# Rows of seven tiles turned and added by DMAs instead of TensorE and VectorE

## The chip, the cores and the metric

One Trainium2 chip, one of its cores. The metric is the device time of one execution of the whole program in microseconds, as the median of several runs.

## What is computed

The input `x` is 128 by 128 by 128 (batch, node, feature). Two residual blocks follow one another, each `layernorm(x + f(x))` over the last axis, with no gain or shift. The first `f` is a two-layer graph network with batch norms. The second `f` mixes the nodes twice with `adj`, and then runs LSTMs over windows of the node axis:

```python
for p in range(1, MAX_SKIP + 1):          # p = 1, 2, 3, 4
    nw = Tv // p
    wins = h[:, :nw * p, :].reshape(Bv * nw, p, Hd)
    last = _lstm_last(Wih[p - 1], Whh[p - 1], bih[p - 1], bhh[p - 1], wins)
    idx = jnp.arange(nw) * p + (p - 1)
    h = h.at[:, idx, :].set(last.reshape(Bv, nw, Hd))
return h
```

So each period p overwrites every p-th row of `h`, and what period 4 leaves is added to the residual, normalized over the 128 features and written.

## The kernel before, in words

The first 400 us compute the first block and the two graph layers of the second. This case is about what follows. The LSTM is cut into 129 units, each one step `s` of a tile of four windows of a period `p` (`Unit(p, tile, s)`). A unit has 512 columns (a few have 256), three gates if it is the first step, else four. The order of the units is a list written out by hand (`LATE`, L84), and every engine walks the same list by slot number `n`:

- **TensorE** (L851 to L854): per gate three matmuls of 512 columns for the input and three more for the state (weights and values are split into a high and a low half in half precision), L678 to L692, into a ring of six banks. Behind unit `n` come the turns that the table `TURNS` gives for slot `n`.
- **ScalarE** (L986 to L988): the gates of unit `n` (L919), then the tanh of its cell (L926).
- **VectorE** (L1296 to L1323): the low half of unit n-1 (L1164), the cell of unit `n` (L1140 for a first step, else L1143, L1145, L1147), the end work that `ADDS` and `MOMENTS` give for slot `n`, then the hidden state (L1154) and its high half (L1159). Each instruction waits in this order.

The values of the last period end up in `hist`: features on the partitions, and for each of 128 times and 128 batch entries a high and a low half in half precision. The output wants the batch on the partitions, so the rows have to be turned. The end is done in 8 tiles of 16 times. Of every four times in a tile, three (`r` = 0, 1, 2) are not rewritten by period 4, so they can be taken as soon as periods 2 and 3 have written them; the fourth (`r` = 3) is the result of the tile's last unit `4.tile.3`. Per tile and `r`, four times are handled at once:

```python
nc.tensor.matmul(acc, hist[:, 0, t, :], ident16[:], start=True, stop=False)
done = nc.tensor.matmul(acc, hist[:, 1, t, :], ident16[:], start=False, stop=True)
```

These are L820 and L821, four times each, into bank 6 or 7 (for `r` = 3 four transposes at L818). VectorE then adds the bank to the residual rows in the tile's buffer (`end_add`, L1227), takes statistics of each row (`end_row_stats`, L1234) and, when the three first rows or the fourth are complete, turns them into mean and variance (`end_moments`, L1177 to L1184). GpSimd follows in the order of `MOMENT_ORDER`: a power for the reciprocal deviation (L545), then a subtract and multiply per row of 128 (L555), 12 rows for the piece `(tile, 0)` and 4 for `(tile, 3)`. The two last pieces, of tiles 6 and 7, are scaled by VectorE (L1253). SyncE writes each piece when it is scaled (L487) and, as there are six tile buffers for eight tiles, loads tiles 6 and 7 when tiles 0 and 1 are written (L472).

`ln_slots` (L159) lays this out. In slots, the end work of before stands at:

```
turns (0,0..2) 61-63   (2,0..2) 76-78    (1,0..2) 80-82    (3,0..2) 89-91
      (4,0..2) 97-99   (5,0..2) 110-112  (6,0..2) 116-118  (7,0..2) 120,121,123
      (0,3) 96  (1,3) 108  (3,3) 114  (2,3) 115  (4,3) 122  (5,3) 126  (6,3) (7,3) 128
add, statistics: one slot behind the turn
```

## Time and profile before

| | |
|---|---|
| median of 3 runs | 754.97 us (754.64 to 755.01) |
| the profiled execution's own time | 754.89 us |
| its span, first to last instruction | 753.1 us |
| TensorE busy | 736.5 us (98%) |
| VectorE busy | 658.2 us (87%) |
| ScalarE busy | 537.7 us (71%) |
| GpSimd busy | 316.5 us (42%) |

The profiled execution's time is 1.8 us more than its span, for what lies around the first and last instruction. The page counts a matmul as busy until its modelled end, and matmuls are pipelined, so a busy share of TensorE doesn't tell by itself whether it waits; its timeline and the list of waits do.

### The profile page before, as it was taken

What the parts mean: (1) busy time and instruction counts of PE and PEld (TensorE: products, weight loads), DVE (VectorE), ACT (ScalarE), POOL (GpSimd) and SP (SyncE); (2) the same over time, 40 slices, a digit from 0 to 9 for tenths busy, and PEclk for the clock granted to TensorE, in tenths of its full rate; (3) what the DMA queues carried; (4) which work ended last, traced back from release to release, by engine and by line L of the source; (5) the groups of instructions that cost most, each with busy time, mean ns of one, the idle gap of its engine ahead of it and who ended that gap; (6) DMA issues with size and microseconds to landing.
All of it is one profiled execution on the core that took longest, in us unless ns stands there. A gap on an engine that the chain in (4) does not pass through costs nothing.

```text
span 753.1 us, 11475 instructions
## 1 busy us (share of the span) xinstructions
PE 736.5 (98%) x3996; PEld 425.2 (56%) x3996; DVE 658.2 (87%) x1400; ACT 537.7 (71%) x870; POOL 316.5 (42%) x286
## 2 busy tenths in 40 slices
PE   8999999999999999998999999999999999999994
PEld 7777544777777677673444444444444444554542
DVE  6888787899898999758998799889999898899987
ACT  4877998567778677659888686786676767666652
POOL 1000000168788787800000002600981946239986
PEclk9999999999999999999999999999999999999997
DMA  5642400033423324105200000100100121021012
GB/s 160 189 140 86 112 2 0 1 83 86 113 77 93 105 65 112 31 28 221 114 1 2 0 1 1 43 0 1 39 34 14 43 70 43 1 70 57 14 57 84
DMA packets 64605, 45.06 MB, mean 60 GB/s; under 512 B 1658, under 2 KB 63524, under 8 KB 63524
## 3 DMA queue, kind: packets, MB, share of 16 engines
q1 hardware_dynamic: 64548, 44.33, 19.2%
q8 instruction: 32, 0.52, 0.3%
q14 instruction: 25, 0.20, 0.1%
HBM read 27.55 MB, written 16.78 MB: 59 GB/s over the span
## 4 chain that ended last, share of the span: by engine, by line
PE 71%; DVE 18%; ACT 7%; issue 2%; SPq 1%; DMA 0%; POOL 0%; POOLq 0%; DVEq 0%
PE ps L678 10%; PE ps L687 10%; PE ps L679 10%; PE ps L646 7%; PE ps L683 7%; PE ps L692 7%; PE ps L684 7%; ACT work L919 4%; PE ps L585 4%; DVE ln_stats L1190 3%; DVE ring L1171 2%; DVE store L1218 2%; DVE ring L1207 2%; PE ps L602 2%; PE ps L601 2%
## 5 line engine op out<-in xcount | busy, mean ns | idle before, releaser
L919 ACT ACTIVATE work<-ps,gate_bias 128x512 f32<-128x512 f32 x449 | 282.6, 680 | 91.4 <-PE ps L692 57.6
L678 PE MATMUL ps<-store,wih 128*128 128x512 f16 (+1 forms) x443 | 166.7, 376 | 2.3 <-ACT work L919 2.3
L679 PE MATMUL ps<-store,wih 128*128 128x512 f16 (+1 forms) x443 | 166.7, 376 | 0.0
L687 PE MATMUL ps<-store,wih 128*128 128x512 f16 (+1 forms) x443 | 156.0, 376 | 0.0
L545 POOL TENSOR_TENSOR end_mv<-end_mv,minus_half 128x12 f32<-128x12 f32 (+1 forms) x16 | 31.0, 1940 | 256.0 <-DVE end_mv L1184 256.0
L536 POOL TENSOR_SCALAR ring<-ring,ln_mv 128x128 f32<-128x128 f32 x112 | 113.0, 1021 | 2.8 <-POOL ln_mv L524 2.7
L1154 DVE TENSOR_TENSOR work<-work 128x512 f32<-128x512 f32 (+1 forms) x129 | 88.2, 684 | 22.4 <-ACT work L926 22.4
L926 ACT ACTIVATE work<-store 128x512 f32<-128x512 f32 x97 | 60.5, 623 | 53.0 <-DVE store L1147 36.4
L683 PE MATMUL ps<-store,whh 128*128 128x512 f16 (+1 forms) x248 | 93.2, 376 | 0.0
L684 PE MATMUL ps<-store,whh 128*128 128x512 f16 (+1 forms) x248 | 93.1, 376 | 0.0
L692 PE MATMUL ps<-store,whh 128*128 128x512 f16 (+1 forms) x248 | 93.0, 376 | 0.0
L555 POOL TENSOR_SCALAR ring<-ring,end_mv 128x128 f32<-128x128 f32 x72 | 85.7, 1202 | 1.4 <-POOL end_mv L545 1.4
L1164 DVE TENSOR_TENSOR store<-work,store 128x512 f16<-128x512 f32 (+1 forms) x121 | 81.9, 677 | 1.4 <-ACT store L952 1.4
L678 PEld LDWEIGHTS ps<-store,wih 128*128 128x128 f16 x443 | 43.3, 98 | 53.1 <-issue 8.2
L687 PEld LDWEIGHTS ps<-store,wih 128*128 128x128 f16 x443 | 43.3, 98 | 50.9 <-DVE store L1164 0.3
L679 PEld LDWEIGHTS ps<-store,wih 128*128 128x128 f16 x443 | 43.3, 98 | 48.3 <-issue 5.0
L519 POOL TENSOR_TENSOR bn_rstd<-mean_var,minus_half 128x1 f32<-128x1 f32 x3 | 1.7, 555 | 133.6 <-DVE mean_var L1098 77.2
L555 POOL TENSOR_SCALAR store<-store,end_mv 128x128 f32<-128x128 f32 x48 | 55.0, 1157 | 1.1 <-POOL end_mv L545 1.1
L870 ACT ACTIVATE store<-ps,vec 128x512 f32<-128x512 f32 x64 | 40.4, 684 | 13.4 <-PE ps L591 13.4
L1143 DVE TENSOR_TENSOR work<-work 128x512 f32<-128x512 f32 (+1 forms) x62 | 42.3, 683 | 8.5 <-ACT work L919 7.5
L1145 DVE TENSOR_TENSOR store<-work,store 128x512 f32<-128x512 f32 (+1 forms) x62 | 42.2, 680 | 7.4 <-ACT work L919 7.2
L1057 DVE BATCH_NORM_STATS2 st<-store 128x6 f32<-128x512 f32 x64 | 41.1, 684 | 8.5 <-ACT store L870 8.3
(136 smaller groups left out, 1284.4 us busy)
## 6 DMA issues: line engine op xcount, KB each, us to landing
ring<-in_x_dram SPq DMA_DIRECT2D x32, 256.0 KB, 3.0
ring<-in_x_dram SPq DMA_DIRECT2D x16, 512.0 KB, 5.3
x_scratch<-ring SPq DMA_DIRECT2D x16, 512.0 KB, 3.5
ring<-x_scratch SPq DMA_DIRECT2D x5, 1024.0 KB, 4.8
out_dram<-ring SPq DMA_DIRECT2D x5, 768.0 KB, 3.5
store<-x_scratch SPq DMA_DIRECT2D x3, 1024.0 KB, 14.1
out_dram<-store SPq DMA_DIRECT2D x3, 768.0 KB, 3.5
out_dram<-ring SPq DMA_DIRECT2D x5, 256.0 KB, 2.3
```

The source lines that it names most:

```text
L536: last = nc.gpsimd.tensor_scalar(row, row, mv[:, 1, b:b + 1], mv[:, 4, b:b + 1], ALU.subtract, ALU.mult)
L555: last = nc.gpsimd.tensor_scalar(row, row, mv[:, 1, k:k + 1], mv[:, 4, k:k + 1], ALU.subtract, ALU.mult)
L678: nc.tensor.matmul(acc(j), w_hi, x_hi, start=True, stop=False)
L679: nc.tensor.matmul(acc(j), w_lo, x_hi, start=False, stop=False)
L683: nc.tensor.matmul(acc(j), w_hi, h_hi, start=False, stop=False)
L684: nc.tensor.matmul(acc(j), w_lo, h_hi, start=False, stop=False)
L687: last = nc.tensor.matmul(acc(j), weights(wih, j)[0], x_lo, start=False, stop=u.first)
L692: nc.tensor.matmul(acc(j), weights(whh, j, 1)[0], h_lo, start=False, stop=True)\
L919: nc.scalar.activation(acts[:, n % 2, gate, 0:u.cols], ps[:, gate_bank(q), 0:u.cols], ACT.Tanh if gate == G else ACT.Sigmoid, bias=gate_bi ...
L926: nc.scalar.activation(tanh_c[:, n % 2, 0:UNITS[n].cols], unit_cell(n), ACT.Tanh)\
L1154: nc.vector.tensor_tensor(hid, hid, tanh_c[:, n % 2, 0:u.cols], ALU.mult).then_inc(hid_done, 1)
L1164: nc.vector.tensor_tensor(unit_output(u, 1), columns(acts[:, n % 2, O, :], u), unit_output(u, 0), ALU.subtract).then_inc(lo_done, 1)
```

## The change

The rows 0 to 2 of tiles 0 to 6 (`MOVED`) no longer go over TensorE and VectorE. For each such tile SyncE issues eight DMAs with a transpose, two halves times four groups of three times, each of 128 by 384 numbers in half precision, into a buffer `h_rows`. It waits for the units that write the rows and for both adds of the tile moved before. GpSimd waits for the four DMAs of the high half and issues a DMA that adds them to the tile's rows, waits for the four of the low half and for its first adding DMA, and issues a second one. VectorE's statistics wait for both.

`h_rows` lies over `minus_c` and `u1_bias`, which only the graph layers use; the buffer for the three is one bank larger. The slots of after:

```
move 0..6 at 59, 69, 76, 83, 92, 99, 113     add (GpSimd) one slot later
statistics (0,0..2) 68-70    (1,0..2) 78-80    (2,0..2) 85-87    (3,0..2) 92-94
           (4,0..2) 101-103  (5,0..2) 108,110,111   (6,0..2) 119-121
turns      (7,0..2) 120,121,123, and the fourth rows where they were
```

GpSimd and SyncE now walk the slots too. In a slot GpSimd first issues the adds and then does the powers and scalings, so the adds of tile 1 stand ahead of the scaling of tile 0 (both slot 70), those of tile 2 (77) ahead of tile 1's (80), those of tile 3 (84) ahead of tile 2's (87), those of tile 4 (93) ahead of tile 3's (94). SyncE issues the writes of a piece four slots behind its statistics (`OUT_DELAY`), behind that slot's moves. The 12 rows of the piece `(6, 0)` are scaled by ScalarE, four each behind the tanh of slots 123, 124 and 125; GpSimd only computes their power and the product of mean and reciprocal deviation, with the mean's sign turned.

```diff
+MOVED = range(P // T_TILE - 1)
+ROWS_ADDED, STATS_DELAY = 6, 9
...
+        start = max(written + 1, start + ROWS_ADDED + 1)
+        put(moves, start, tile)
+        put(lands, start + 1, tile)
+        wanted.append((start + (STATS_DELAY if tile < MOVED[-1] else ROWS_ADDED) - 1, tile))
...
+OUT_DELAY = 4
+BY_SCALARE, BY_VECTOR = [(6, 0)], MOMENTS[len(UNITS) - 1]
+POOLED = [piece for piece in MOMENT_ORDER if piece not in BY_SCALARE and piece not in BY_VECTOR]
+SCALES = {max(n for n in STATS if (6, 2) in STATS[n]) + 2 + r: (6, r) for r in range(3)}
...
-        minus_c = sb("minus_c", [P, CB, P])
-        u1_bias = sb("u1_bias", [P, CB, P])
+        turned = sb("turned", [P, 3 * BANK])
+        minus_c, u1_bias = (turned[:, k * BANK:(k + 1) * BANK].rearrange("p (b n) -> p b n", b=CB) for k in range(2))
+        h_rows = turned[:].bitcast(F16).rearrange("p (s k d) -> p s k d", s=2, d=P)
...
+            def move_rows(tile):
+                n = MOVE_ORDER.index(tile)
+                sp.wait_ge(lo_done, halves_through(max(NUMBER[v] for v in sources(Unit(4, tile, 0)))))
+                wait(sp, h_added, 32 * n)
+                for s in range(2):
+                    for m in range(CB):
+                        t = tile * T_TILE + 4 * m
+                        sp.dma_start(h_rows[:, s, 3 * m:3 * m + 3, :],
+                                     hist[:, s, t:t + 3, :].rearrange("p t b -> p (t b)"),
+                                     transpose=True).then_inc(h_moved[s], 16)
...
+            for n in range(N_EARLY, len(UNITS) + OUT_DELAY):
+                for tile in MOVES.get(n, ()):
+                    move_rows(tile)
+                for piece in MOMENTS.get(n - OUT_DELAY, ()):
+                    write_rows(piece)
...
+            def add_rows(tile):
+                n = MOVE_ORDER.index(tile)
+                rows = first_rows(x1_tile[tile % X1_RING])
+                pool.wait_ge(x1_loaded[tile % X1_RING], 16 * (tile // X1_RING + 1))
+                for s in range(2):
+                    pool.wait_ge(h_moved[s], 16 * CB * (n + 1))
+                    wait(pool, h_added, 16 * (2 * n + s))
+                    nc.gpsimd.dma_start(rows, h_rows[:, s, :, :].rearrange("p (m r) d -> p m (r d)", r=3), accum_op=ALU.add).then_inc(h_added, 16)
...
+                if piece in BY_SCALARE:
+                    nc.gpsimd.tensor_tensor(mv[:, 2, cols], mv[:, 1, cols], mv[:, 4, cols], ALU.mult)\
+                        .then_inc(end_offset, 1)
+                    return
...
+            for n in range(N_EARLY, len(UNITS)):
+                for tile in LANDS.get(n, ()):
+                    add_rows(tile)
+                for piece in MOMENTS.get(n, ()):
+                    scale_rows(piece)
...
+            def end_scale(tile, r):
+                piece = (tile, 3 if r == 3 else 0)
+                act.wait_ge(end_offset, BY_SCALARE.index(piece) + 1)
+                for m in range(CB):
+                    row = x1_tile[tile % X1_RING][:, 4 * m + r, :]
+                    k = r * CB + m
+                    last = nc.scalar.activation(row, row, ACT.Identity, bias=end_mv[:, tile, 2, k:k + 1],
+                                                scale=end_mv[:, tile, 4, k:k + 1])
+                if r == moment_rows(piece).stop - 1:
+                    last.then_inc(end_scaled_act, 1)
...
             for n in range(N_GROUPED, len(UNITS)):
                 gates(n)
                 tanh_cell(n)
+                if n in SCALES:
+                    end_scale(*SCALES[n])
...
-                dve.wait_ge(end_added, ADD_ORDER.index((tile, r)) + 1)
+                if (tile, r) in TURN_ORDER:
+                    dve.wait_ge(end_added, TURN_ORDER.index((tile, r)) + 1)
+                else:
+                    dve.wait_ge(h_added, 32 * (MOVE_ORDER.index(tile) + 1))
...
-                    for tile, r in ADDS.get(n, ()):
-                        end_add(tile, r)
+                    for tile, r in STATS.get(n, ()):
+                        if (tile, r) in TURN_ORDER:
+                            end_add(tile, r)
                         end_row_stats(tile, r)
```

## Rows read from the trace of the kernel before

**Rows 1.** The page, part 1: busy us (share of the span) and instructions of each engine.
```profile
PE 736.5 (98%) x3996; PEld 425.2 (56%) x3996; DVE 658.2 (87%) x1400; ACT 537.7 (71%) x870; POOL 316.5 (42%) x286
```

**Rows 2.** Stages: us, busy (count) of PE PEld DVE ACT POOL, PEclk, DMA, GB/s.
```profile
448.00:550.00 102.00, 102.00 (x522) 48.20 (x520) 94.20 (x190) 72.21 (x115) 40.37 (x30) 1.00 0.05 16
550.00:650.00 100.00, 100.00 (x521) 48.90 (x519) 88.72 (x176) 69.62 (x113) 53.18 (x41) 1.00 0.11 38
650.00:741.00 91.00, 91.00 (x497) 45.68 (x495) 84.12 (x208) 57.12 (x92) 71.55 (x60) 1.00 0.13 41
sum 293.00, PE 293.00 PEld 142.78 DVE 267.03 ACT 198.96 POOL 165.11; mean PE 97.67 PEld 47.59 DVE 89.01 ACT 66.32 POOL 55.04
```

**Rows 3.** Timeline of TensorE: start us, duration us, line, operation, count.
```profile
450.70 0.38 PE L692 MATMUL ps<-store,whh 128*128 128x512 f16 x1
450.91 0.22 PE L820 MATMUL ps<-ident,store 128*128 128x128 f16 x1
...
451.36 0.38 PE L678 MATMUL ps<-store,wih 128*128 128x512 f16 x1
...
741.33 0.60 PE L818 MATMUL ps<-ident,work 128*128 128x128 f32 x4
```

**Rows 4.** List of waits from 440 us: who waited for whom, us, times, longest.
```profile
PE ps L818 <- DVE work L1154: 2.5, 1, 2.5
...
PEld ps L692 <- DVE store L1164: 0.4, 2, 0.2
```

**Rows 5.** Groups by line from 440 us: count | busy us, mean ns | idle before.
```profile
L555 POOL TENSOR_SCALAR ring<-ring,end_mv 128x128 f32<-128x128 f32 x72 | 85.7, 1202 | 1.4 <-POOL end_mv L545 1.4
...
L1227 DVE TENSOR_TENSOR ring<-ps,ring 128x512 f32<-128x512 f32 x20 | 13.6, 681 | 0.0
L820 PE MATMUL ps<-ident,store 128*128 128x128 f16 x96 | 13.3, 219 | 0.0
L821 PE MATMUL ps<-ident,store 128*128 128x128 f16 x96 | 13.3, 219 | 0.0
```

**Rows 6.** Timeline of GpSimd and of SyncE's queue.
```profile
466.12 2.66 POOL L545 TENSOR_TENSOR end_mv<-end_mv,minus_half 128x12 f32<-128x12 f32 x1 [147.07 <-DVE end_mv L1184]
468.96 14.06 POOL L555 TENSOR_SCALAR ring<-ring,end_mv 128x128 f32<-128x128 f32 x12 [0.18 <-POOL end_mv L545]
...
483.05 0.39 SPq L487 DMA_DIRECT2D out_dram<-ring  x1
...
662.05 0.34 SPq L472 DMA_DIRECT2D ring<-x_scratch  x1
```

**Rows 7.** DMA issues: count, KB each, median us from issue to landing.
```profile
store<-x_scratch SPq DMA_DIRECT2D x3, 1024.0 KB, 14.1
out_dram<-store SPq DMA_DIRECT2D x3, 768.0 KB, 3.5
...
work<-in_L_gnn_bg_dram SPq DMA_DIRECT2D x1, 64.0 KB, 3.0
```

**Rows 8.** Timeline of VectorE: starts of the cells of units 69, 85, 92, 108, 121.
```profile
483.31 0.69 DVE L1143 TENSOR_TENSOR work<-work 128x512 f32<-128x512 f32 x1 [0.43 <-ACT work L919]
...
546.97 0.69 DVE L1143 TENSOR_TENSOR work<-work 128x512 f32<-128x512 f32 x1
...
577.35 0.69 DVE L1140 TENSOR_TENSOR store<-work 128x512 f32<-128x512 f32 x1
...
644.84 0.69 DVE L1143 TENSOR_TENSOR work<-work 128x512 f32<-128x512 f32 x1 [1.15 <-ACT work L919]
...
703.80 0.69 DVE L1143 TENSOR_TENSOR work<-work 128x512 f32<-128x512 f32 x1
```

**Rows 9.** ScalarE's L941, from 147 us: ns min/median/max.
```profile
L941 ACT ACTIVATE ring<-ring,ln_mv x14: 477/479/494, 147.0 to 155.1; 128x128 f32<-128x128 f32 x14
```

**Rows 10.** Timeline of ScalarE and VectorE, units 126 to 128.
```profile
728.27 1.85 ACT L919 ACTIVATE work<-ps,gate_bias 128x512 f32<-128x512 f32 x3
...
735.06 0.69 ACT L919 ACTIVATE work<-ps,gate_bias 128x512 f32<-128x512 f32 x1 [0.46 <-PE ps L692]
...
737.25 0.68 DVE L1164 TENSOR_TENSOR store<-work,store 128x512 f16<-128x512 f32 x1
```

More of the change, by code:

```diff
@@ L156, in scaled_through @@
     return scaled_rows(min(g, 1), 7) + max(g - 1, 0)
+MOVED = range(P // T_TILE - 1)
+ROWS_ADDED, STATS_DELAY = 6, 9
 def ln_slots():
-    turns, adds, moments = {}, {}, {}
+    moves, lands, turns, stats, moments = {}, {}, {}, {}, {}
     end = len(UNITS) - 1
@@ L170, in ln_slots @@
         fixed[NUMBER[Unit(4, tile, 3)] + 1] = tile
-    wanted = []
+    wanted, start = [], 0
     for tile in range(P // T_TILE):
-        ready = max(NUMBER[v] for v in sources(Unit(4, tile, 0))) + 2
-        wanted.append((max(ready, NUMBER[Unit(4, tile, 0)]), tile))
-    places, free = [(at, (tile, 3)) for at, tile in fixed.items()], 0
+        written = max(NUMBER[v] for v in sources(Unit(4, tile, 0)))
+        if tile not in MOVED:
+            wanted.append((max(written + 2, NUMBER[Unit(4, tile, 0)]), tile))
+            continue
+        start = max(written + 1, start + ROWS_ADDED + 1)
+        put(moves, start, tile)
+        put(lands, start + 1, tile)
+        wanted.append((start + (STATS_DELAY if tile < MOVED[-1] else ROWS_ADDED) - 1, tile))
+    places, free = [(at, (tile, 3)) for at, tile in fixed.items()], {}
     for at, tile in sorted(wanted):
         for r in range(3):
-            at = max(at, free)
+            at = max(at, free.get(tile in MOVED, 0))
             while at in fixed:
@@ L357, in resnorm_gnn_kernel @@
         x1_loaded = [sem(f"x1_loaded{k}") for k in range(X1_RING)]
+        h_moved = [sem(f"h_moved{s}") for s in range(2)]
+        h_added = sem("h_added")
+        end_offset, end_scaled_act = sem("end_offset"), sem("end_scaled_act")
         h_turned, end_added, end_stats_done, end_step, end_var, end_rstd, end_scaled, tail_scaled = (
@@ L1212, in bias_u1 @@
                 nc.vector.tensor_tensor(u1[:, h * CB:(h + 1) * CB, :].rearrange("p b n -> p (b n)"), ps[:, U1[h], :],
[L1213 removed]
+                                        turned[:, BANK:2 * BANK], ALU.add).then_inc(u1_copied, 1)
             def gnn_lo(g):
@@ L1238, in end_moments, with end_scale @@
                 tile, rows = piece[0], moment_rows(piece)
[L1239 removed]
+                dve.wait_ge(end_stats_done, CB * (STAT_ORDER.index((tile, rows.stop - 1)) + 1))
                 cols = slice(rows.start * CB, rows.stop * CB)
                 moments(end_stats[:, tile % 2, :, :, :].rearrange("p r m s -> p (r m) s")[:, cols, :],
[L1242 to L1244 removed]
+                        end_mv[:, tile, :, cols], end_step, 4 * n, end_var,
+                        sign=-1.0 if piece in BY_SCALARE else 1.0)
+            def end_scale(tile, r):
+                piece = (tile, 3 if r == 3 else 0)
                 n = MOMENT_ORDER.index(piece)
[L1246 removed]
                 dve.wait_ge(end_step, 4 * (n + 1))
                 dve.wait_ge(end_rstd, n + 1)
[L1249 to L1255 removed]
+                for m in range(CB):
+                    row = x1_tile[tile % X1_RING][:, 4 * m + r, :]
+                    k = r * CB + m
+                    last = nc.vector.tensor_scalar(row, row, end_mv[:, tile, 1, k:k + 1],
+                                                   end_mv[:, tile, 4, k:k + 1], ALU.subtract, ALU.mult)
+                if r == moment_rows(piece).stop - 1:
+                    last.then_inc(tail_scaled, 1)
             residual(0, 0)
@@ L1309, in _ @@
                 else:
-                    for tile, r in ADDS[end][:-1]:
+                    for tile, r in STATS[end][:-1]:
                         end_add(tile, r)
@@ L1314, in _ @@
                     hidden_hi(n)
-            for tile, r in ADDS[end]:
-                if (tile, r) == ADDS[end][-1]:
+            for tile, r in STATS[end]:
+                if (tile, r) == STATS[end][-1]:
                     end_add(tile, r)
@@ L1321, in _ @@
                         end_moments(piece)
-            for piece in TAIL:
-                end_scale(piece)
+            for tile, r in TAIL:
+                end_scale(tile, r)
 DEG_STEP = 9
```

52 lines of the change are left out of this document (22 added, 30 removed).

## The prediction

> **What bounds the kernel now.** I read the page first, for shares: TensorE is busy for 98% of the span, VectorE for 87% [rows 1]. A share is an average, so the next view is the table by stage over 448 to 741 us, the only stretch that the change touches: TensorE is busy without a break in every stage, at a granted clock of 1.00, which is the 2.4 GHz level, while VectorE stands at 89 to 92% and ScalarE at 63 to 71% [rows 2]. A busy TensorE may still hide waits, so I then read its own timeline: matmuls of 512 columns start every 0.215 us, and next to them a turned row takes its place in the same row of starts, from 450.91 us to the next gate matmul at 451.36 us [rows 3]. The list of waits confirms it: from 440 us on TensorE's matmuls waited once, for 2.5 us, and that is the last turn of all, behind the final unit; its weight loads waited for tenths [rows 4]. So in this stretch the end moves by what leaves TensorE's stream, one for one, as long as the other engines still deliver on time. Behind 741.33 us stand the tail of turn, add, statistics, power, scaling and write, 11.8 us, which the change leaves as it is.
>
> **What is removed.** Seven tiles times three rows are 21 turns, each of eight matmuls of 128 columns. L820, one of their two lines, counts 96 for eight tiles (L821 the same), so 84 of each go [rows 5]. One turn costs 451.36 - 450.91 = 0.45 us, and 21 of them 9.4 us. (Not eight times the mean of the group, 219 ns: that holds the pipeline's latency, the distance of starts is the price.) On VectorE the 21 adds from PSUM go, of 0.68 us each: 14.3 us [rows 5]. That shortens no sum by itself, since VectorE isn't the bound, but it loses more than TensorE does, so it stays ahead. Tile 7, the fourth rows of all tiles and all statistics stay.
>
> **What is added on SyncE.** Per tile eight transposing DMAs of 96 KB. No transposing DMA stands in the trace, so I bound one: from below by the issue of a plain one, 0.39 us; from above by a whole landing of a 64 KB transfer, 3.0 us, as if each waited for the last [rows 6, 7]. I take i = 1.5 us, between the two, as a descriptor stream that turns data should cost more than an issue and a queue should hide part of the landing: 12 us a tile. What else SyncE does is now threaded between them: each tile's write comes at the earliest four slots behind its statistics, and tile 6's eight transposes (12 us) stand ahead of a write and of tile 7's load, which was issued at 662.05 us for a use behind 703.80 us [rows 6, 8]. Even 12 us later and landing in 14.1 us it is 15 us early. So this queue has a price only if turned rows land late.
>
> **What is added on GpSimd.** Per tile two adding DMAs from half to single precision into the tile. Each moves 768 KB of destination in and out. The nearest row is the 768 KB write, landed after 3.5 us; the farthest the 1,024 KB load that queued behind others, 14.1 us [rows 7]. I take 5 us, and 1 us of GpSimd for each issue (bounds: the 0.39 us issue and the 2.66 us of its power instruction [rows 6]). GpSimd waits in place, first for the turned rows, then for the first add; behind it stand the power and scaling of the tile before, 2.66 + 0.18 + 14.06 = 16.9 us [rows 6], and behind that on SyncE the write of that tile and the next tile's move. This is the one loop that can become late, and its tightest case is tile 2. Tile 1's move starts when unit 68 is written, inside slot 69: its cell starts at 483.31 us [rows 8], less three removed turns (1.3), plus 2.5 us of that slot's VectorE work, 484.5 us. Then eight transposes (8i), landing (2), the second issue (1), scaling of tile 0 (16.9), its write's issue (0.4), eight transposes (8i), landing (2), the second add (5): tile 2 is complete at 511.8 + 16i. VectorE wants it in slot 85: 546.97 us [rows 8], less nine turns (4.0), plus 2.1 us of cell work, 545 us. So it is in time while i is below (545 - 511.8) / 16 = 2.1 us; at i = 1.5 it is 9 us early. Tile 5 repeats the pattern from 577.35 us to 644.84 us [rows 8]: 577.35 - 5.4 + 2.5 + 27.3 + 16i against 644.84 - 6.7 + 2.1, so i up to 2.4 us. Tiles 0, 1, 3 and 4 don't wait for a scaling ahead of their move, or do so with more room. So at i = 1.5 the cost is nothing, and the cover is these 9 us.
>
> How the Trainium skill prices it stands by itself. "VectorE: DVE Perf Modes", The three transpose paths, gives a 128 by 128 block of two-byte numbers 390 ns on TensorE and 1,309 ns through the DMA crossbar, which speaks against this change: three such blocks one after another would be 3.9 us a DMA, far above 2.1. "DMA: Bandwidth & Descriptors", Latency and other measured facts, gives 261 GB/s for transposing DMAs, by which 96 KB would be 0.4 us, far below. No row here decides between them.
>
> **What is added on ScalarE.** Tile 6's 12 rows, four behind the tanh of each of slots 123 to 125. The same instruction at L941 took 0.479 us [rows 9], so 1.9 us a slot, 5.7 us in all. In the last of them ScalarE would end at 730.2 us instead of 728.3; the three gates that took it 1.85 us from 728.27 us [rows 10] and the fourth then run back to back to 732.8. By the gate at 735.06 us it is still some 0.6 us late. That gate leads to the cell of unit 127 and, behind it, to the low halves at 737.25 us [rows 10], for which the weight load of TensorE's last unit waits already, 0.2 us of the 0.4 that L692 waits for L1164 [rows 4]: 0.6 us comes back onto the path. TensorE's six banks hide the rest. GpSimd loses those 12 rows (14.4 us at 1.20 us each [rows 5]), which pays for part of its new waits.
>
> **The sum.** -9.4 + 0.6 = -8.8 us against the profiled execution, 754.89 us with a span of 753.1 us: 746.1 us. The median shown is 754.97 us, 0.08 above it, so the forecast is 746.2 us. 0.2% (1.5 us) is about what a measurement of this kernel can tell from no change.
>
> **Rivals.**
> 1. *The turned rows come late.* It decides from i = 2.1 us on. Each further 0.1 us holds tile 2 by 1.6 us, as VectorE waits in its own order and TensorE runs dry after its six banks. At the upper bound i = 3.0 tile 2 is late by 511.8 + 48 - 545 = 15 us, tile 5 by 10 to 16, tiles 4 and 6 by a few: some 38 us against 9.4 gained, so about 783 us. For it: two queues take turns in one loop, and GpSimd, busy for 165 of 293 us already, is held for most of the rest. Against it: bigger plain transfers are issued in 0.39 us [rows 6], and the DMA engines are busy for 5 to 13% [rows 2]. Chance 0.15. (The skill's 1,309 ns a block, from "VectorE: DVE Perf Modes", would be this rival at i = 3.9: tile 2 alone 29 us late, the time above 800 us, as an estimate. It is part of the 0.15.)
> 2. *Part of the gain is given back.* The chain gate, cell, tanh, hidden, halves becomes the bound here and there once TensorE's stream is denser: VectorE's 92% of 448 to 550 us leaves 7.8 us of 102 [rows 2]; or i is 2.1 to 2.4 and tile 2 or 5 holds VectorE for 1 to 5 us. 748 to 752 us. For it: the low halves of unit 126 already come a little late [rows 4, 10]. Against: VectorE loses 14.3 us, TensorE 9.4. Chance 0.15.
> 3. *Nothing comes of it.* The end is held by something that the turns only filled. Against it stands a TensorE without a gap from 448 to 741 us [rows 2, 4]. About 755 us, chance 0.04.
>
> The forecast has 0.66, from 745.3 (no ScalarE price) to 747.5 us.
>
> **How the numbers follow.** Faster by over 0.2%: the forecast and the second rival, 0.81. Within: 0.04. Slower: 0.15. The range goes from 744.6 us, a turn's price with the rounding of its starts (0.45 against 0.43 to 0.48), to 752 us, the far end of the second rival; the slow rival and the empty one, 2 in 10, are left out.
>
> **What the profile after should show.** L820 and L821 x12 each; L1227 x11; TensorE's stretch without a gap, ending at about 732.5 us instead of 741.33; 56 transposing DMAs issued by SyncE at under 2.1 us each; no wait of VectorE's statistics (L1234) for a DMA; ScalarE's 12 new instructions at 0.48 us; the tail again 11.8 us. Wrong would be: statistics that wait for GpSimd's DMA in slots 85 or 108, TensorE idle behind it, or a granted clock below 1.00 in a stage.

## The result, and the profile after

| | before | after |
|---|---|---|
| median (range, runs), us | 754.76 (754.64 to 755.3, 7) | 751.98 (748.01 to 752.72, 7) |
| the profiled execution's own time | 754.89 us | 748.24 us |
| its span | 753.1 us | 746.4 us |

The ratio of the means is 0.9946, with a 95% interval of 0.9935 to 0.9956: 4.1 us faster (2.8 us by the medians), where 8.6 us were forecast. And there is no single time after: executions lie anywhere from 748.0 to 752.7 us, while those of before agree within 0.7 us. The profile of after comes from one of the fastest, so it shows only part of the loss; profiles of the slower ones were taken later.

The page of after, part 1, answers [rows 1], and the stages answer [rows 2] (columns as there).

```profile
PE 726.6 (97%) x3828; PEld 414.8 (56%) x3828; DVE 644.1 (86%) x1379; ACT 540.2 (72%) x882; POOL 315.2 (42%) x289
```
```profile
448.00:550.00 102.00, 101.94 (x473) 45.95 (x472) 91.83 (x180) 76.22 (x121) 37.84 (x28) 1.00 0.41 81
550.00:650.00 100.00, 100.00 (x486) 47.40 (x484) 87.16 (x192) 68.51 (x111) 67.69 (x57) 1.00 0.47 106
650.00:741.00 91.00, 83.75 (x428) 40.93 (x426) 80.41 (x205) 58.37 (x101) 64.01 (x55) 0.99 0.32 84
```

168 matmuls and 21 VectorE instructions went, so the change does what it says. The DMA engines, busy for 5 to 13% before, stand at 32 to 47%. TensorE's last unit is done earlier by 741.33 - 734.64 = 6.7 us [rows 3], which is the whole gain of the span, and the tail behind it is 11.8 us as before:

The timeline of TensorE of after (columns as in [rows 3]).

```profile
702.18 0.66 PE L878 MATMUL ps<-ident,work 128*128 128x128 f32 x4 [2.14 <-DVE work L1227]
...
734.64 0.60 PE L878 MATMUL ps<-ident,work 128*128 128x128 f32 x4
```

21 turns at 0.45 us would be 9.4 us. Adding up the gaps between starts of TensorE's rows from 448 to 734 us gives 2.6 us (0.23 near 504 us, 2.30 at 702.18 us, 0.06 elsewhere), and 9.4 - 2.6 = 6.8. So everything that was removed came, and in this execution one gap took most of the loss. The waits of after from 440 us answer [rows 4].

```profile
PE ps L878 <- DVE work L1227: 4.6, 2, 2.4
...
DVE end_stats L1310 <- DMA ring<-turned: 3.1, 2, 2.9
...
DVE end_stats L1310 <- DMA store<-turned: 1.1, 1, 1.1
```

The first line holds the old wait of the last turn (2.45 us) and the new one of 2.14 us. The others are what the prediction called the sign of an error: statistics that wait for GpSimd's adding DMA (the profile names the tile's buffer now ring, now store). Its place is in the timeline of VectorE of after, the first statistics of tiles 2 (slot 85) and 6 (slot 119), and the hidden state behind them.

```profile
543.18 0.87 DVE L1310 BATCH_NORM_STATS2 end_stats<-ring 128x6 f32<-128x128 f32 x4 [0.28 <-DMA ring<-turned]
...
691.18 0.87 DVE L1310 BATCH_NORM_STATS2 end_stats<-ring 128x6 f32<-128x128 f32 x4 [2.86 <-DMA ring<-turned]
...
701.44 0.68 DVE L1227 TENSOR_TENSOR work<-work 128x512 f32<-128x512 f32 x1
```

Follow the 2.86 us back. The timelines of SyncE's queue and of GpSimd and, in the last line, the chain of waits of after:

```profile
663.67 11.73 SPq L510 DMA_TRANSPOSE turned<-store  x8
...
675.45 1.35 SPq L522 DMA_DIRECT2D out_dram<-ring  x1
...
679.70 0.34 SPq L493 DMA_DIRECT2D ring<-x_scratch  x1
```
```profile
672.27 1.26 POOL L588 DMA_DIRECT2D ring<-turned  x1
...
679.36 1.28 POOL L588 DMA_DIRECT2D ring<-turned  x1 [5.82 <-DMA turned<-store]
```
```profile
679.36 11.80 DMA ring<-turned
```

Tile 6's second add is issued at 679.36 us, tile 7's load of 1 MB at 679.70 us. A write of 768 KB is issued right behind, at 680.09 us. The add lands after 11.8 us. The stage says how full the 16 DMA engines are (0.91, at 240 GB/s):

```profile
680.00:692.00 12.00, 12.00 (x63) 5.72 (x62) 8.45 (x17) 8.16 (x13) 10.96 (x11) 1.00 0.91 240
```

VectorE is 2.86 us late in slot 119 and has two more statistics to do in slots 120 and 121, so the hidden state of unit 121, which tile 4's last turn reads, comes late, and TensorE waits for it.

### The profile page after: what moved, and what is told of

Same layout as the page of the kernel before. It is cut to its first block, busy times and chain, and to the rows that moved or that the text cites. A ratio compares the mean times of both kernels' runs of the same rounds, so it can differ in the third digit from the quotient of the medians.

```text
span 746.4 us, 11167 instructions
## 1 busy us (share of the span) xinstructions
PE 726.6 (97%) x3828; PEld 414.8 (56%) x3828; DVE 644.1 (86%) x1379; ACT 540.2 (72%) x882; POOL 315.2 (42%) x289
## 4 chain that ended last, share of the span: by engine, by line
PE 60%; DVE 21%; ACT 7%; DMA 4%; SPq 3%; issue 3%; POOL 0%; POOLq 0%; DVEq 0%
PE ps L739 8%; PE ps L740 8%; PE ps L748 8%; PE ps L707 7%; PE ps L744 5%; PE ps L753 5%; PE ps L745 5%; ACT work L979 4%; PE ps L646 4%; DVE ln_stats L1263 3%; SPq L510 3%; DVE work L1227 2%; DVE store L1291 2%; DVE ring L1244 2%; DVE ring L1280 2%
## 5 line engine op out<-in xcount | busy, mean ns | idle before, releaser
L588 POOL DMA_DIRECT2D ring<-turned x8 | 10.6, 1319 | 198.5 <-DMA turned<-store 190.5
L610 POOL TENSOR_SCALAR ring<-ring,end_mv 128x128 f32<-128x128 f32 x60 | 71.3, 1200 | 1.3 <-POOL end_mv L596 1.3
L610 POOL TENSOR_SCALAR store<-store,end_mv 128x128 f32<-128x128 f32 x48 | 50.6, 1066 | 1.1 <-POOL end_mv L596 1.1
```

Of the source, the lines that this page charges most:

```text
L610: last = nc.gpsimd.tensor_scalar(row, row, mv[:, 1, k:k + 1], mv[:, 4, k:k + 1], ALU.subtract, ALU.mult)
```

## The experiments

Differences of one microsecond matter here, so each kernel has 4 to 6 runs beside those of the kernel before, except where fewer are named. All medians are in us.

### The changed kernel again, and the DMAs alone taken out

r1_again and r2_again are the changed kernel as it is.

> The changed kernel once more, unedited. Its seven times lie in two heaps, 748.0 to 749.5 us and 752.0 to 752.7 us, and only one of the first heap has a trace. Theory A (late rows: the statistics of tiles 2, 5 and 6 wait for the adding DMAs, whose landing varies): where the time is near 752 us the profile shows VectorE's statistics waiting some 4 us longer in total than the 4.2 us seen, and a longer hole in TensorE. Theory B (ScalarE's twelve scalings hold the last gates): the time near 752 us shows the same waits for DMAs and more idle TensorE in slots 124 to 128. Theory C (the chain gate, cell, hidden state is too slow for the denser stream): small gaps all over. Median between 748 and 752.7 us by all three.

Measured: 750.92 (750.25 to 752.54, 5), ratio 0.9945 (0.9933 to 0.9958), span 749.3. Its profile shows more of what that of after shows: the statistics of tile 5 in slot 108 wait 4.1 us and not 1.1. Slots 124 to 128 have no gap, and small gaps all over aren't there either, so theories B and C have nothing for them. One part of theory A is wrong: the landing doesn't vary. Tile 5's second add takes 9.3 us in after and 9.6 in r1_again; what differs is when it is issued. r2_again ran later:

> The changed kernel, unedited, beside the mended ones on one chip: 748 to 752.7 us, 2.5 to 6 us above loads apart in every run.

Measured: 749.19 (748.05 to 753.64, 6), ratio 0.9931 (0.9912 to 0.995). One run lies above the range and no run between 750.03 and 753.64 us.

e1_no_moves takes out both kinds of DMA and the waits for them:

```diff
-                wait(sp, h_added, 32 * n)
...
-                        sp.dma_start(h_rows[...], hist[...], transpose=True).then_inc(h_moved[s], 16)
...
-                for s in range(2):
-                    pool.wait_ge(h_moved[s], 16 * CB * (n + 1))
-                    wait(pool, h_added, 16 * (2 * n + s))
-                    nc.gpsimd.dma_start(rows, h_rows[...], accum_op=ALU.add).then_inc(h_added, 16)
...
-                    dve.wait_ge(h_added, 32 * (MOVE_ORDER.index(tile) + 1))
+                        dve.wait_ge(x1_loaded[tile % X1_RING], 16 * (tile // X1_RING + 1))
```

> The 56 transposing and 14 adding DMAs are left out, with the waits for them, so seven tiles' first three rows miss their LSTM part; everything else stands as in the changed kernel. This is the ceiling of the change. Theory A: TensorE has no hole from 448 us to its last unit, VectorE's statistics wait for nothing, the whole 9.4 us come, less at most 0.6 for ScalarE: 745.3 to 746.1 us, and the times lie in one heap within 0.5 us. Theory B: 748 us or more, with the loss in slots 124 to 128. Theory C: 748 us or more, with gaps all over.

Measured: 746.26 (746.18 to 746.85, 4), ratio 0.9884 (0.9869 to 0.9899), span 744.1. From 440 us on TensorE's matmuls wait once, for the last turn (waits of e1_no_moves), and the last stage is full again at a DMA share of 0.14:

```profile
PE ps L867 <- DVE work L1216: 2.5, 1, 2.5
```
```profile
650.00:732.00 82.00, 82.00 (x419) 40.10 (x418) 72.93 (x178) 56.80 (x97) 55.93 (x47) 1.00 0.14 46
```

The whole loss lies in the DMAs or in what waits for them, and the spread over several us is gone with them. That 746.26 us meets the forecast of 746.2 us to the tenth is partly luck: the forecast holds 0.6 us for ScalarE that no gap shows, and 0.4 us of this time lies outside the span (746.28 - 744.1 = 2.2 us in its profile, where before has 1.8).

### Which DMA, and beside what

e4_small_loads leaves the moves and the adds and shrinks the loads of tiles 6 and 7:

```diff
-                    load_x1(tile + X1_RING)
+                    late = tile + X1_RING
+                    sp.dma_start(x1_tile[late % X1_RING][:, 0:1, :], x1_dram[:, late * T_TILE:late * T_TILE + 1, :])\
+                        .then_inc(x1_loaded[late % X1_RING], 16)
```

> Tiles 6 and 7 load one of their sixteen rows (64 KB instead of 1,024 KB), so the rest of their residual is missing; nothing else is changed. Theory A1 (the second adding DMA of tiles 5 and 6 is slow because it shares the DMA engines with these two loads, issued 1.2 us and 0.3 us beside it): the second adds of tiles 5 and 6 land in 6 to 7 us instead of 9.3 and 11.8, the waits of slots 108 and 119 shrink from 1 to 4 and 2.9 us to under 1 us each, the hole of 2.3 us goes: 746.5 us, within 0.5 of the kernel without moves (746.26). Rival A2 (the adds are slow because GpSimd issues them late, behind its scalings, and transposes and writes load the engines): both waits stay over 1 us, time over 748 us.

Measured: 745.67 (745.6 to 745.78, 4), ratio 0.9875 (0.9859 to 0.9892). Tile 6's second add alone, from issue to landing (view by source line), and the load beside it (DMA issues from 660 to 700 us, columns as in [rows 7]), after and then e4_small_loads:

```profile
DMA to landing us min/median/max: 11.8/11.8/11.8
...
ring<-x_scratch SPq DMA_DIRECT2D x1, 1024.0 KB, 6.1
```
```profile
DMA to landing us min/median/max: 7.6/7.6/7.6
...
ring<-x_scratch SPq DMA_DIRECT2D x1, 64.0 KB, 1.9
```

Tile 6's second add takes 7.6 us and not 11.8, tile 5's 5.7 and not 9.3, and of the statistics' waits one of 0.3 us is left. Nothing but the two loads was made smaller, and all adds, moves and writes stayed.

e5_loads_apart does it with the whole computation: each late load goes where no add is under way. For that the writes come one slot earlier too (`OUT_DELAY`), so this run by itself doesn't tell the loads from the writes; e4_small_loads, which leaves the writes in their slots, does.

```diff
-OUT_DELAY = 4
+OUT_DELAY = 3
...
-                if piece[1] == 3 and tile + X1_RING < TILES:
+                if piece[1] == 3 and 0 < tile < TILES - X1_RING:
...
+                if n == 109:
+                    sp.wait_ge(h_added, 32 * 6)
+                    sp.wait_ge(out_written[0], 32)
+                    load_x1(X1_RING)
```

> The two loads are moved away from the adds: tile 6's waits for tile 5's second add, tile 7's is issued ahead of tile 6's move instead of behind it, as each piece is written three slots behind its statistics instead of four. A1: the same as with small loads, at most 0.5 us above it: 746.5 to 747 us, one heap. A2: no change from the changed kernel, 748 to 752.7 us. A load that is late would show as a wait of the adds in slot 121 for a DMA from the scratch tensor.

> Loads apart, unedited, once more beside the next version: 745.5 to 746.0 us, with a run near 748.7 us now and then. If the rare late one comes from the loop on SyncE's queue, it is missing from the version with moves first.

Measured: 745.74 (745.55 to 748.7, 4) and, as e10_apart_again, 745.88 (745.76 to 746.45, 4), ratios 0.9886 (0.9867 to 0.9905) and 0.9882 (0.9869 to 0.9894). The timeline of SyncE's queue of e5_loads_apart has tile 7's load ahead of tile 6's move, tile 6's second add lands after 5.7 us (view by source line), and TensorE ends its last unit at 732.01 us, 9.3 before 741.33:

```profile
658.09 0.34 SPq L493 DMA_DIRECT2D ring<-x_scratch  x1
...
662.25 12.39 SPq L510 DMA_TRANSPOSE turned<-store  x8
```
```profile
DMA to landing us min/median/max: 5.7/5.7/5.7
```
```profile
732.01 0.60 PE L882 MATMUL ps<-ident,work 128*128 128x128 f32 x4
```

All 9.3 us are there with all DMAs. The price was not the number of these DMAs, but the moment at which they met. Of the 6.1 us by which tile 6's second add was slow (11.8 against 5.7), 4.2 go with the load. The other 1.9 are there in e4_small_loads too, where the write of 768 KB still follows the add after 0.35 us; in e5_loads_apart that write is issued 3.8 us ahead of it. The one run at 748.7 us has no counterpart in e10_apart_again, nor in the four of e8_moves_first below, and no profile; where it came from stays open.

### Why the times differ from run to run

m1_again, m2_again and m3_again are the changed kernel again, one run each, for their profiles.

> The changed kernel, unedited, for one more trace. If its time is above 751 us: with theory A the waits for DMAs in slots 85, 108 and 119 sum to 8 us or more and TensorE's holes to 6 us or more; if a hole is over some 4 us, the matmuls behind it start every 0.43 us for a few us, a granted clock of half.

> As m1_again: below 749 us the waits sum to 4 to 5 us with one hole of 2.3 to 2.8 us; above 751 us to 8 us or more.

> As m1_again: below 749 us the waits sum to 4 to 5 us with one hole of 2.3 to 2.8 us; above 751 us to 8 us or more.

Measured: 751.22, 752.52 and 752.84. The waits of m1_again and of m2_again show the one in slot 108 that was 1.1 us in after:

```profile
DVE end_stats L1310 <- DMA store<-turned: 4.1, 1, 4.1
...
DVE end_stats L1310 <- DMA ring<-turned: 3.6, 2, 3.4
```
```profile
DVE end_stats L1310 <- DMA store<-turned: 3.6, 1, 3.6
```

The waits sum to 7.7 us in m1_again and 7.2 in m2_again, a little under the 8 us expected. The one in slot 108 is for tile 5's second add, which in after is issued at 632.91 us and lands after 9.3 us, beside tile 6's load (issued at 634.07 us). Timelines of GpSimd and of SyncE's queue ahead of it, of after, then of m2_again:

```profile
604.21 13.11 POOL L610 TENSOR_SCALAR store<-store,end_mv 128x128 f32<-128x128 f32 x12 [0.18 <-POOL end_mv L596]
...
625.30 1.36 POOL L588 DMA_DIRECT2D store<-turned  x1 [2.79 <-issue]
...
632.91 1.29 POOL L588 DMA_DIRECT2D store<-turned  x1 [6.25 <-DMA turned<-store]
```
```profile
617.35 0.37 SPq L522 DMA_DIRECT2D out_dram<-store  x1
617.82 13.68 SPq L510 DMA_TRANSPOSE turned<-store  x8
```
```profile
604.48 13.91 POOL L610 TENSOR_SCALAR store<-store,end_mv 128x128 f32<-128x128 f32 x12 [0.18 <-POOL end_mv L596]
...
627.82 1.35 POOL L588 DMA_DIRECT2D store<-turned  x1 [3.47 <-issue]
```
```profile
618.42 0.37 SPq L522 DMA_DIRECT2D out_dram<-store  x1
618.89 12.42 SPq L510 DMA_TRANSPOSE turned<-store  x8
```

Tile 3's 12 rows are all scaled at 617.32 us in after and at 618.39 in m2_again, for a longer power (2.84 and 3.30 us) and longer scalings (13.11 and 13.91). The write behind them and tile 5's move behind the write come 1.1 us later with them. But tile 5's first add is issued 2.5 us later, and the second 2.2.

The difference is made on the way: GpSimd is idle ahead of the first add in both, for 2.8 and 3.5 us, as it waits for the move's first four DMAs (the profile says "issue"). In after the fourth of the eight is issued at 622.38 us and lands after 2.4 us; in m2_again it is issued at 623.45 and lands after 3.8. The profiles with this move at its place all have one such DMA, issued between 623.3 and 624.0 us (in e7_both at 624.58) and landing after 3.8 to 4.2 us. Where the move starts from 617.4 to 618.1 us (after, r2_again, e3_six_tiles, e5_loads_apart, e10_apart_again, e2_pool_scales_6; in e7_both too), that is the fifth or the sixth and the first add goes out at 624.9 to 625.6 us. Where it starts from 618.8 to 619.1 us (r1_again, the three m runs, e4_small_loads, e11_apart_pool), it is the fourth, and the add goes out at 627.8 to 628.3 us. So about 1 us of lateness of GpSimd becomes 2.5 us by a step, and the times lie in heaps.

What makes one DMA land late is in the traces too. Each profile has a transfer of 16 KB on a queue that it names "instruction", at 625.1 to 625.9 us (in e7_both at 626.4). The DMA queues of m2_again from 625 to 626 us (queue, kind: packets, MB, share of the 16 engines):

```profile
q8 instruction: 1, 0.02, 6.8%
```

Counted over the 16 profiles that have transposing DMAs: of 347 such DMAs with neither an add, a write or a load nor a transfer of instructions in their time, all landed after 2.3 to 2.7 us; of 64 with only a transfer of instructions, 55 landed after 3.0 to 4.3 us. No run moves such a transfer, so that it is the cause is argued and not shown. And e4_small_loads and e11_apart_pool are at the late place and lose nothing by it: with no load beside it, tile 5's second add takes 5.7 us.

In the slower runs TensorE then has a gap of 1.4 (m2_again) or 1.9 us (m1_again) at 646 us and smaller ones at 648 and 671 us. Gaps in all: after 2.6 us, m1_again 5.6, m2_again 5.2; 9.4 less these is 6.8, 3.8 and 4.2, against spans that fell by 6.7, 3.7 and 2.4. In after and m1_again that closes. (The gaps, too, stay a little under the 6 us expected.) In m2_again 1.8 us are missing, and most of them are the clock: behind the gap of slot 119 (2.9 us in both) the stage shows a granted clock of 0.51, the 1.2 GHz level, for 3.5 us, with 11 matmuls where m1_again has 18, and 7 times 0.215 us is 1.5. m1_again and then m2_again, and the timeline of TensorE of m2_again (starts 0.43 us apart, not 0.215):

```profile
705.00:708.50 3.50, 3.33 (x18) 1.79 (x19) 3.43 (x10) 1.11 (x2) 2.46 (x2) 1.00 0.01 2
```
```profile
705.00:708.50 3.50, 3.50 (x11) 1.59 (x11) 3.43 (x9) 0.63 (x1) 2.12 (x2) 0.51 0.01 2
```
```profile
705.59 0.63 PE L739 MATMUL ps<-store,wih 128*128 128x512 f16 x1
706.02 0.63 PE L740 MATMUL ps<-store,wih 128*128 128x512 f16 x1
```

So the profiled runs are near 748 us with the gap of slot 119 alone, at 751 with that of slot 108 besides, and above 752 where the clock falls as well. (m3_again is like m2_again.) Why GpSimd takes 1 us longer in some runs stays open. e3_six_tiles leaves tile 6 on TensorE:

```diff
-MOVED = range(P // T_TILE - 1)
+MOVED = range(P // T_TILE - 2)
...
-        wanted.append((start + (STATS_DELAY if tile < MOVED[-1] else ROWS_ADDED) - 1, tile))
+        wanted.append((start + STATS_DELAY - 1, tile))
```

> Only tiles 0 to 5 are moved, tile 6 is turned by TensorE and added by VectorE as before (slots 116 to 119); ScalarE still scales its rows. Three turns come back, 1.3 us. Theory A: the 2.3 us hole behind slot 119 is gone, so it is 1 us faster than the changed kernel's fast heap, 747 us, and if tile 6 makes the two heaps, one heap is left; if tiles 2 and 5 make them, both stay, at 747 and up to 751 us. Theory B and C: 1.3 us slower than the changed kernel.

Measured: 749.91 (747.52 to 750.41, 5), ratio 0.992 (0.9905 to 0.9934). Slot 119 is gone as a place, slot 108 isn't: its runs lie at 747.5 to 747.7 or at 749.9 to 750.4, which the account above has as the two places of tile 5's first add; only a run at 747.52 has a profile.

### More room for the rows

e6_stats_later puts the statistics of tiles 0 to 4 one slot later and those of tile 5 two, e7_both adds that to e5_loads_apart:

```diff
-ROWS_ADDED, STATS_DELAY = 6, 9
+ROWS_ADDED, STATS_DELAY = 6, 10
```

> The statistics of tiles 0 to 4 come one slot later, those of tile 5 two slots (110 to 112). The loads stay beside the adds. All theories under A: the waits of slots 85 and 108 vanish. But tile 5's moments come 4 us later, GpSimd scales tile 5 until some 676 us instead of 672.3 and issues tile 6's first add behind that, so the wait of slot 119 grows from 2.9 to 5 us or more and the hole with it: 749 to 752 us, one heap, if the two heaps come from slot 108; two heaps still, if they come from slot 119.

> Loads apart and statistics later together. A1: 746.5 to 747.5 us, one heap: tile 6's second add lands in 6 to 7 us, which makes up for GpSimd's later scaling of tile 5. A2: 749 us or more.

Measured: 746.88 (746.72 to 747.29, 4) and 746.26 (746.06 to 746.56, 4), ratios 0.9892 (0.9878 to 0.9907) and 0.9884 (0.9869 to 0.9899). e6_stats_later did better than I had reckoned: the later statistics moved a write behind move 5 as well, and the wait in slot 119 shrank to 1.1 us. With the loads apart the later slot gains nothing (746.26 against 745.74).

e8_moves_first is e5_loads_apart with the 12-row pieces written six slots behind their statistics, so that no move stands behind a write that waits for GpSimd:

```diff
-            for n in range(N_EARLY, len(UNITS) + OUT_DELAY):
+            for n in range(N_EARLY, len(UNITS) + 6):
...
                 for piece in MOMENTS.get(n - OUT_DELAY, ()):
-                    write_rows(piece)
+                    if piece[1] == 3:
+                        write_rows(piece)
+                for piece in MOMENTS.get(n - 6, ()):
+                    if piece[1] == 0:
+                        write_rows(piece)
```

> As loads apart, and the writes of the twelve-row pieces come six slots behind their statistics, so that tile 2's move no longer stands behind tile 0's write on SyncE's queue, nor tile 5's behind tile 3's. Theory A with the loop (move, add, GpSimd's scaling, write, move): tile 2's transposes start near 508 us instead of 520.9 and its first add is issued right behind GpSimd's scaling, near 520.5 us instead of 528.4; tiles 2 and 5 land 6 us or more earlier; no statistics wait for a DMA, all times within 0.5 us: 745.7 us, as with loads apart, whose one time in four near 748.7 us does not come back. If GpSimd alone set the landing, tiles 2 and 5 would land as before.

Measured: 745.81 (745.59 to 745.96, 4), ratio 0.9879 (0.9864 to 0.9893). No statistics wait at all, and tile 2's adds (timeline of GpSimd of e8_moves_first) stand right behind the scaling, with no time spent on waiting for turned rows:

```profile
520.38 1.33 POOL L596 DMA_DIRECT2D ring<-turned  x1
...
528.15 1.28 POOL L596 DMA_DIRECT2D ring<-turned  x1 [6.44 <-DMA ring<-turned]
```

That cuts the loop in two and is the version with the most room; by time it can't be told from e5_loads_apart. Both beat both kernels, before and after.

### The price of a transposing DMA in the loop

e9_more_moves issues 14 of them per tile, the six more into spare buffers, and computes the same:

```diff
                                      transpose=True).then_inc(h_moved[s], 16)
+                        if m < 3:
+                            sp.dma_start(h_spare[3 * s + m], hist[:, s, t:t + 3, :]..., transpose=True).then_inc(h_moved[s], 16)
...
-                    pool.wait_ge(h_moved[s], 16 * CB * (n + 1))
+                    pool.wait_ge(h_moved[s], 16 * 7 * (n + 1))
```

> The changed kernel with 14 transposing DMAs a tile instead of 8; the six more write their turned rows where nothing reads them. At 1.55 us each that is 21.7 us a tile instead of 12.4. The loop counts this twice for tiles 2 and 5: with 16i as in the prediction they come 18.6 us later than now, waits of 19 us in slot 85 and 20 us in slot 108, 2 to 4 us for tiles 3 and 4 and some 12 us for tile 6, less a microsecond or two of banks each: about 795 us. Without the loop (transposes only beside GpSimd's work) each tile would be 9.3 us later, less its cover: about 768 us.

Measured: 781.93 (2 runs), ratio 1.0358 (1.034 to 1.0375). The waits of e9_more_moves:

```profile
DVE end_stats L1318 <- DMA store<-turned: 20.1, 3, 17.1
DVE end_stats L1318 <- DMA ring<-turned: 19.8, 2, 12.7
```

The time lies midway between the 795 us expected with the loop and the 768 without it, so it doesn't decide; the timelines do. Tile 2 waits 12.7 us, tile 5 17.1. From tile 1's move to its second add it is 22.3 us instead of 15.45, for tile 2 22.2 instead of 16.03, with GpSimd's work between them 0.4 us shorter: 6.8 + 6.2 - 0.4 = 12.6 us, the added DMAs twice. So the loop is real, and a helping is 6.2 to 6.8 us and not the 9.3 us expected. The rest of the miss is TensorE: its gap is 7.2 us behind the wait of 12.7 and 14.8 behind that of 17.1, so the banks took more than the microsecond or two allowed. All its gaps sum to 29.1 us, and the half clock behind three of them costs 7.0: 753.1 - 9.4 + 29.1 + 7.0 = 779.8, for a span of 780.0 us. This is the prediction's first rival, called up at will.

### ScalarE or GpSimd for tile 6's rows

e2_pool_scales_6 gives them back to GpSimd, e11_apart_pool does so in e5_loads_apart:

```diff
-BY_SCALARE, BY_VECTOR = [(6, 0)], MOMENTS[len(UNITS) - 1]
+BY_SCALARE, BY_VECTOR = [], MOMENTS[len(UNITS) - 1]
...
-SCALES = {max(n for n in STATS if (6, 2) in STATS[n]) + 2 + r: (6, r) for r in range(3)}
+SCALES = {}
```

> Tile 6's first rows are scaled by GpSimd again, as before; all else as changed. Theory A: the hole in TensorE lies ahead of slot 123 and comes from slot 119's wait, so it stays: within 0.7 us of the changed kernel either way, two heaps as there. Theory B: faster by 1 us or more and one heap. It can lose if GpSimd is late for the powers of the tail, which come 2.7 + 13 us later on its queue: then a power of slots 123 to 128 waits.

> Loads apart, but GpSimd scales tile 6's first rows again. Those 12 rows take it 13 to 14 us from some 701 us on, and the power and scaling of (4,3) and (7,0) come behind them, so the powers of the tail come late: as with late rows, VectorE's last scaling waits some 3 us for a power and the tail behind TensorE is 14.5 to 15 us instead of 11.8. 748.5 to 749 us. If ScalarE's part is worth nothing: 745.7 us; if it costs what the prediction said: 745.1 us.

Measured: 751.75 (751.07 to 754.1, 5), ratio 0.9959 (0.9946 to 0.9972), of which the spread of the changed kernel leaves little to read (its profile has the same 3.0 us in the tail as the one below); and 748.49 (748.39 to 748.97, 5), ratio 0.9913 (0.99 to 0.9927), which nothing swallows: 2.7 us more than e5_loads_apart. TensorE ends as early, but in the tail VectorE waits for the power of the last rows, for which GpSimd had no time (waits of e11_apart_pool from 700 us):

```profile
DVE ring L1333 <- POOL end_mv L600: 3.0, 1, 3.0
```

## Why the prediction was right, and where it was wrong

**What is removed: right.** 9.4 us for 21 turns; e5_loads_apart gives 9.3 us of span. The distance of starts was the price of a turn.

**ScalarE's 12 rows: wrong in size and sign.** The instructions took what was forecast, as the groups of after show, but no gap of TensorE follows them in slots 124 to 128, so the 0.6 us are 0. (The prediction's working doesn't give them either: no row leads from its 732.8 us to the gate at 735.06.) And the prediction counted their use only as a part payment for GpSimd's waits: it is the 3.0 us of tail that e11_apart_pool loses without them.

```profile
L1052 ACT ACTIVATE ring<-ring,end_mv 128x128 f32<-128x128 f32 x12 | 4.9, 478 | 0.0
```

**A transposing DMA: i was right.** Forecast 1.5 us, measured 11.7 to 13.7 us for eight (1.46 to 1.7), and 1.3 us where nothing else is under way. All of them, in the view by tile, and their landing, in the DMA issues, of after:

```profile
L510 SPq DMA_TRANSPOSE turned<-store x56: 1180/1257/2898, 444.2 to 673.5; - x56
```
```profile
turned<-store SPq DMA_TRANSPOSE x56, 2.4
```

The bounds of 0.39 and 3.0 us held it. The Trainium skill's figure of 1,309 ns for a 128 by 128 block ("VectorE: DVE Perf Modes", The three transpose paths) isn't borne out as a price per block in a row of them: three blocks took 1.30 us. Nor are the 261 GB/s of the Trainium skill ("DMA: Bandwidth & Descriptors", Latency and other measured facts) reached by these DMAs: 96 KB in 1.30 us are 75 GB/s. What a DMA costs until its rows can be used is another term: the prediction took 2 us for the last one's landing behind its issue. A DMA with nothing beside it lands after 2.4 us from its start. The eighth of tiles 1 and 2, with the tile's own first add under way, lands after 5.5 and 5.9 us from its start, 3.5 and 3.0 us behind the end of its issue.

**The cover: this is the step that failed, in three places.** The prediction summed tile 2's loop to 511.8 + 16i, so 535.8 us against 545 us, and concluded: "So at i = 1.5 the cost is nothing, and the cover is these 9 us." But the cost was not nothing: TensorE stood idle for 2.6 us in after and for 5.6 in m1_again, behind statistics that waited for tiles 2, 5 and 6. Tile 2 first, on the loop's own rows in after (SyncE, then GpSimd, then SyncE, then GpSimd):

```profile
485.24 11.68 SPq L510 DMA_TRANSPOSE turned<-store  x8
```
```profile
500.69 1.29 POOL L588 DMA_DIRECT2D ring<-turned  x1 [5.81 <-DMA turned<-store]
...
504.66 15.75 POOL L610 TENSOR_SCALAR ring<-ring,end_mv 128x128 f32<-128x128 f32 x12 [0.19 <-POOL end_mv L596]
...
536.96 1.28 POOL L588 DMA_DIRECT2D ring<-turned  x1 [7.23 <-DMA turned<-store]
```

| step of tile 2 | forecast, us | measured, us |
|---|---|---|
| start of tile 1's move | 484.5 | 485.24 |
| eight DMAs, landing, to its second add | 14.0 | 15.45 |
| issue, power, scaling, write, to tile 2's move | 18.3 | 20.24 |
| eight DMAs, landing, to its second add | 14.0 | 16.03 |
| the second add | 5.0 | 6.2 |
| complete | 535.8 | 543.2 |
| wanted | 545 | 542.9 |

Every term was a little too small, and none by much: 7.4 us together. The want was too late by 2.1 us: VectorE's cell of slot 85 starts 6.8 us earlier than before (540.15 us against 546.97) and not the 4.0 of nine turns, as nine adds of 0.68 us have left VectorE too. 9.2 - 7.4 - 2.1 = -0.3, and the statistics wait 0.28 us. A cover that one sums from seven estimates has to bear the errors of all seven; and yet in this place, called the tightest, the loss stayed at 0.3 us. The larger losses lie in the other two.

**Tiles 5 and 6: never worked out to the end.** At i = 1.5 the prediction's own formula has tile 5 complete at 625.8 us and wanted at 640.2, so 14.5 us early. Measured in after it is complete at 642.2 and wanted at 641.2, and the statistics wait 1.1 us. The largest error, 9.3 us, is a term put at nothing: tiles 0, 1, 3 and 4 "don't wait for a scaling ahead of their move, or do so with more room". Tile 4's move was to start at 574.5 us and started at 583.79, right behind a write that waited for GpSimd's scaling of tile 2, done at 583.29 us (timeline of SyncE's queue of after):

```profile
583.32 0.37 SPq L522 DMA_DIRECT2D out_dram<-ring  x1
583.79 12.60 SPq L510 DMA_TRANSPOSE turned<-store  x8
```

In e8_moves_first, where no such write stands ahead, it starts at 573.15 us. From there to tile 5's second add the errors are +2.6, -0.9 and +1.1 us, and the add itself, 9.3 us instead of 5, is the second largest: 9.3 + 2.6 - 0.9 + 1.1 + 4.3 = 16.4 us.

Tile 6 wasn't summed at all. It misses by the add alone: issued at 679.36 us and wanted at 688.32, it was in time with anything up to 9.0 us and took 11.8. The prediction asked whether tile 7's load would itself be late ("it is 15 us early"; it landed at 685.82 us for a use at 699.37) and not what it does to the add issued 0.34 us before it. So the 5 us for an add is the mis-sized term behind tile 6's wait and a part of tile 5's: the second adds of tiles 5 and 6 take 5.7 to 5.8 us with no load or write issued behind them (e5_loads_apart), tile 6's 7.6 beside a 768 KB write (e4_small_loads), tile 5's 9.3 beside tile 6's load and tile 6's 11.8 beside tile 7's load and that write. The upper bound of 14.1 us, from a load that queued behind others, was in the text and was the better neighbour for an add that has a load beside it.

**The rivals.** The second one, part of the gain given back, is what came, in its range of 748 to 752 us. Of its mechanisms the chain of gates did nothing; tiles 2 and 5 did hold VectorE, though with i at 1.5 and not above 2.1, and tile 6, which it doesn't name, held it most. The first, rows late by tens of us, needs i above 2.1: e9_more_moves makes it, at 14 DMAs of 1.3 us each, which is an i of 2.3 for eight, and gets 781.9 us. The measured median 751.98 lies at the very end of the range, 0.02 us inside it, which is luck: the seven runs average 750.8, and other runs of the same kernel reach 753.64.

**The signs.** "Statistics that wait for GpSimd's DMA in slots 85 or 108, TensorE idle behind it" came true: the waits in both (0.3 us in slot 85, 1.1 to 4.1 in slot 108), gaps behind them, and in slot 119, where the gap is in every profile of the changed kernel. A granted clock below 1.00 inside TensorE's stream came in m2_again and m3_again; the 0.99 of the last stage of after isn't one, as the clock falls there at 739.38 us, behind TensorE's last unit, as before at 744.26. And five of the 56 transposing DMAs held SyncE for more than 2.1 us (up to 2.9), all beside an adding DMA.

## What to carry to other kernels

When work moves to DMAs, list for each new transfer that somebody waits for what other transfers are issued within its time, loads for later tiles first: a load with 13 us to spare cost this kernel 2.3 us or more because it was issued 0.34 us behind an add with 9.0 us to land in. Putting the loads where no add is under way cost nothing and brought everything back. Where a queue issues in order, look also at what stands ahead of a transfer: a write that waits for a slower engine holds every move behind it, here by 9.3 us. Sum a loop across queues with bounds for every term, and compare the sum of the errors with the cover, not each error; a cover of 9 us over a loop of 51 was gone here.

## What the runs showed of the hardware beyond the expected

- An adding DMA (half to single precision, 768 KB of destination) holds GpSimd for 1.26 to 1.48 us. In after it lands after 5.7 to 8.5 us with no load beside it, and after 9.3 and 11.8 us beside one of 1 MB.
- A transposing DMA of 96 KB lands after 2.3 to 2.7 us with nothing beside it, mostly after 3.0 to 4.3 us where a transfer of instructions falls into its time (16 profiles), and after up to 7.6 us with an adding DMA issued behind it (after).
- GpSimd's scaling of 12 rows took 11.3 to 15.9 us at different places of after, and at one place 13.11 us in some runs and 13.91 in others. About 1 us more on GpSimd there, by way of a DMA that landed late, moved the time of the whole kernel by 3 us.
- Behind the gap in slot 119 the granted clock fell to half for 3.4 us in m2_again (a gap of 2.9 us) and m3_again (2.8) and stayed at 1.00 in m1_again (2.9) and r2_again (2.8); I had expected it only behind more than 4 us. In e9_more_moves it fell with the gaps of 4.4, 7.2 and 14.8 us, and matmuls started at half the rate for 3 to 6 us behind them, but not behind one of 2.1 us. In m2_again that made a gap of 2.9 us cost 1.5 us more.
